# Segment sums in the bank of the used-up edge products, and GpSimd's sums in two pieces

## The chip, the cores and the metric
The kernel runs on one core of a Trainium2 chip. The metric is the device time of one execution in microseconds (us); less is better. The engines of the core run side by side, each with a queue of its own that it works off in order: TensorE (PE in the profile, its weight loads PEld), VectorE (DVE), ScalarE (ACT), GpSimd (POOL) and SyncE (SP, which only issues DMAs). They wait for each other by semaphores. PE writes its results to eight banks of PSUM.

## The reference, cut to what matters
Two message-passing layers over 100,000 nodes of 160 numbers (64 scalars, 32 vectors of 3) and 25,000 edges sorted by destination; each layer has a layer norm and a residual. The first layer:

```python
h = relu(layernorm(x))
f, sc = linear(h, lin1), linear(h, sc_w) * node_attr         # per node, 160 wide
w = silu(edge_scalars @ fc_w1) @ fc_w2                        # per edge, 192 weights
edge_feat = products of f[edge_src], edge_attr and w          # per edge, 384 wide
mid = segment_sum(edge_feat, edge_dst, num_segments=N)
x = x + cos(angle(mid)) * sc + sin(angle(mid)) * lin2(mid)
```

The second layer gathers, multiplies, sums by destination and adds `relu` of it to x. Few nodes have edges: for the others the first layer is the dense part alone (x + sc), and the second adds nothing.

## The kernel before, in words
Three passes follow one another.

**Pass 1** does two things at once, woven together slot by slot. The dense part takes the nodes in U = 98 blocks u of 1024 rows (128 partitions, 8 rows each). The edge part takes the edges in T = 196 tiles n of 128, four tiles to a quad q. A step is one dense block with two tiles, and each step has two slots (h = 0 and 1), one tile and half a block in each. The order inside a step is written out by hand for every engine, and each engine runs its own list (`step` and `slot`), so that several blocks and tiles are in flight.

Dense block u, in order:
- SP loads its rows (`x_all`), DVE takes the moments (L1207) and centres them into `hb` (L1330) and `hr` (L1331).
- PE transposes one half of them in each slot (`dense_tr`, L980 and L981, into bank 0 and columns 0 to 127 of bank 1), ACT copies them with relu (`dense_copy`, L795 and L796).
- One step later PE multiplies (`dense_mm`, L985 and L986), DVE forms x1 (L1354) and the second moments, ACT takes the second root (L779), DVE the inverse (L1370) and the shift `nmr` (L1211).
- ACT writes h1 in two halves of four groups each (`dense_h1`, L774). GpSimd adds each half to x1 in `dense_y` (L651, 640 columns), and SP stores h1 and this output.

Edge tile n, in slots s = n, n+1, and so on:
- Slot n: PE forms the source products and the 192 edge weights in bank 5 or 6 by turns (`p1_source`, ends at L1062). ACT scales the first 160 columns out as `g_e` (L824). DVE multiplies features (`p1_features`, L1421 to L1428); one of its products is kept in columns 352 to 447 of the same bank.
- Slot n+1: PE transposes the features (`p1_feat_t`, L1087, bank 4), ACT copies them (L838).
- Slot n+2: PE forms the message parts in bank 7 (L1048 to L1051), ACT and DVE make the message `v_e` of them (L817, L1402, L1409).
- Slot n+3: `p1_sum` sums the messages by destination: two matmuls, one with the tile's selector matrix `same`, one that carries the tile before on (L1075, L1077), 161 columns wide. They go to columns 256 to 416 of bank 1. ACT copies the result to `tot` (`p1_total`, L832).

Once a quad, DVE builds the selector (L1381), GpSimd centres the gathered edge rows (L655, L656) and issues four indirect gathers (L604), PE transposes these rows (`p1_tr`) into bank 4 and columns 128 to 255 of bank 1, and ACT copies them (L811, L812).

So bank 1 is shared by three users: the rest of the dense transposes, the rest of the edge rows' transposes and the segment sums. While ACT reads one of them out, PE does not write another: `dense_tr` and `p1_tr` wait for `e_tot` (the sums' copy), and `p1_sum` waits for `d_hT` (the copy of the dense transposes).

PE's order in a slot is: dense products of the block before, (once a quad `p1_tr`), feature transposes of tile s-1, message parts of s-2, source products of s, sum of s-3, and then the dense transposes.

**Pass 2** gathers the nodes that have edges and redoes their row with the edge part; **pass 3** runs the second layer over the edges. Both come after pass 1.

Of the kernel before, what the change touches and what calls it, by code (L numbers as in the profile page):

```python
# [19 lines left out]
P = 128  # L20
GD = 8
GQ = 4
D = 160
# [4 lines left out]
CW = D + 1  # L28
# [7 lines left out]


U_C, U_A, U_D, U_B = 0, 32, 97, 193
U_SEG = 2 * P


class At:
# [26 lines left out]
def wait(eng, sem, value):  # L69

    if not (isinstance(value, int) and value <= 0):
        eng.wait_ge(sem, value)  # L72


def gnn_kernel(nc, xa, src, dst, dst_rows, number, edges_in, scalars_in, scalars_t_in, wpack, out):
    f32, i32 = mybir.dt.float32, mybir.dt.int32
    ALU, ACT, AX = mybir.AluOpType, mybir.ActivationFunctionType, mybir.AxisListType
    N = xa.shape[0]
    T = src.shape[1]
    Q = T // GQ  # L80
    UROWS = P * GD
    U = -(-N // UROWS)
# [36 lines left out]
    with ExitStack() as ctx:  # L119
# [3 lines left out]
        def two(name, shape, dt=f32):  # L123
            return [sb(f"{name}{i}", shape, dt) for i in range(2)]
# [4 lines left out]
        def sem(name):  # L129
            return ctx.enter_context(nc.semaphore(name))  # L130
# [4 lines left out]
        bank = [ctx.enter_context(nc.psum_tensor(f"bank{i}", [P, 512], f32)) for i in range(8)]  # L135
# [49 lines left out]
        x1 = two("x1", [P, GD * D])  # L185
        h1 = two("h1", [P, GD * D])
        yo = two("yo", [P, GD * D])
# [7 lines left out]
        same = two("same", [P, GQ * P])  # L195
        carry = two("carry", [P, GQ * P])
# [11 lines left out]
        v_e = two("v_e", [P, CW])  # L208
        tot = two("tot", [P, GQ * CW])
# [59 lines left out]
        d_hT = sem("dense_hT_copied")  # L269
# [8 lines left out]
        d_y = sem("dense_y_ready")  # L278
# [17 lines left out]
        e_ft = sem("p1_features_ready")  # L296
# [7 lines left out]
        e_tot = sem("p1_sum_copied")  # L304
# [283 lines left out]
        def _(pool):  # L588
# [55 lines left out]
            def dense_y(u):  # L644
                j = u.mod(2)
                for h in range(2):
                    pool.wait_ge(d_h1, u.times(2, h + 1))
                    if h == 0:
                        wait(pool, d_sto[j], u.over(2, 16))
                    a, b = h * GQ * D, (h + 1) * GQ * D  # L650
                    nc.gpsimd.tensor_tensor(yo[j][:, a:b], x1[j][:, a:b], h1[j][:, a:b], ALU.add).then_inc(d_y, 1)  # L651

            def centre(into, rest, rows, st, g, signal):
                x = x3(rows, XW, g)
# [111 lines left out]
        def _(act):  # L766
# [60 lines left out]
            def p1_total(n):  # L827
                act.wait_ge(e_seg, n.times(1, 1))
                j, t = n.c // GQ % 2, n.mod(4)
                if t == 0:  # L830
                    wait(act, e_st[j], n.over(8, 16))
                nc.scalar.activation(tot[j][:, t * CW:(t + 1) * CW], bank[1][:, U_SEG:U_SEG + CW],  # L832
                                     ACT.Copy).then_inc(e_tot, 1)

            def p1_feat_t(n):
# [140 lines left out]
        def _(pe):  # L976
            def transpose_rows(main, rest, ps_main, ps_rest, tr_sem):

                for t in range(GQ):
                    nc.tensor.transpose(ps_main[:, t * P:(t + 1) * P], main[:, t * P:(t + 1) * P], ident[:, :])  # L980
                nc.tensor.transpose(ps_rest, rest, ident[:, :]).then_inc(tr_sem, 1)  # L981

            def linear(dst_ps, main, rest, w, t):

                nc.tensor.matmul(dst_ps, main[:, t * P:(t + 1) * P], wp[:, w:w + D], start=True, stop=False)  # L985
                return nc.tensor.matmul(dst_ps[:, 0:DS], rest[:, :], wp[:, w + D + t * DS:w + D + (t + 1) * DS],  # L986
                                        start=False, stop=True)
# [20 lines left out]
            def dense_mm(u, h):  # L1008
                pe.wait_ge(d_hT, u.times(2, h + 1))
                for k in range(GQ):  # L1010
                    if h == 0 and k == 0:
                        pe.wait_ge(d_scl, u.times(1, 1))
                    if k % 2 == 0:
                        wait(pe, d_x1, u.times(4, 2 * h + k // 2 - 1))
                    ins = linear(bank[2 + k // 2][:, k % 2 * D:(k % 2 + 1) * D], hT[h], hR[h], W_SC, k)
                    if k % 2 == 1:
                        ins.then_inc(d_mm, 1)

            def dense_tr(u, h):
                pe.wait_ge(d_cen, u.times(1, 1))  # L1020
                wait(pe, d_hT, u.times(2, h))
                wait(pe, e_tot, u.times(2, h - 2))
                q = At(u.i, u.c // 2, 2) + u.c % 2 * h
                pe.wait_ge(e_hT, q.times(1, 1) if q.within(Q) else Q)
                transpose_rows(hb[u.mod(2)][:, h * 4 * P:(h + 1) * 4 * P], hr[u.mod(2)][:, h * P:(h + 1) * P], bank[0],
                               bank[1][:, 0:P], d_tr)
# [10 lines left out]
            def p1_tr(q):  # L1037
                pe.wait_ge(e_cen, q.times(1, 1))
                wait(pe, e_fte, q.times(GQ, -2))
                wait(pe, d_hT, q.times(4, -1))  # L1040
                wait(pe, e_tot, q.times(4, -4))
                transpose_rows(h_e[:, :], hr_e[:, :], bank[4], bank[1][:, P:2 * P], e_tr)

            def p1_parts(n):
                pe.wait_ge(e_fte, n.times(1, 1))
                wait(pe, e_v, n.times(1))
                f = fT[n.mod(2)]
                nc.tensor.matmul(bank[7][:, U_C:U_C + 97], f[:, 0:P], wp[:, W_R1:W_R1 + 97], start=True, stop=True)  # L1048
                nc.tensor.matmul(bank[7][:, U_D:U_D + 161], f[:, P:2 * P], wp[:, W_R2:W_R2 + 161],
                                 start=True, stop=False)  # L1050
                nc.tensor.matmul(bank[7][:, U_B:U_B + 65], f[:, 2 * P:3 * P], wp[:, W_R3:W_R3 + 65],  # L1051
                                 start=False, stop=True).then_inc(e_u, 1)

            def p1_source(n):
                j, t = n.c // GQ % 2, n.mod(4)
                if t == 0:
                    pe.wait_ge(e_hT, n.over(4, 1, 1))
                    pe.wait_ge(e_hid[j], n.over(8, 16, 16))
                wait(pe, e_ft, n.times(1, -1))
                b = bank[5 + n.mod(2)]  # L1060
                linear(b[:, 0:D], eT[j], eR[j], W_L1, t)
                nc.tensor.matmul(b[:, D:D + 192], q_hid[j][:, t // 2 * P:(t // 2 + 1) * P],  # L1062
                                 wp[:, W_FC2 + t % 2 * 192:W_FC2 + (t % 2 + 1) * 192],
                                 start=True, stop=True).then_inc(e_pw, 1)

            def p1_sum(n, dense_copied):
                j, t = n.c // GQ % 2, n.mod(4)
                if t == 0:
                    pe.wait_ge(e_sc, n.over(4, 1, 1))
                    pe.wait_ge(e_ca[j], n.over(8, 16, 16))  # L1070
                pe.wait_ge(e_v, n.times(1, 1))
                wait(pe, e_tot, n.times(1))
                wait(pe, d_hT, dense_copied)
                before = tot[j][:, (t - 1) * CW:t * CW] if t else tot[1 - j][:, (GQ - 1) * CW:GQ * CW]
                nc.tensor.matmul(bank[1][:, U_SEG:U_SEG + CW], same[j][:, t * P:(t + 1) * P], v_e[n.mod(2)][:, :],  # L1075
                                 start=True, stop=False)
                nc.tensor.matmul(bank[1][:, U_SEG:U_SEG + CW], carry[j][:, t * P:(t + 1) * P], before,  # L1077
                                 start=False, stop=True).then_inc(e_seg, 1)

            def p1_feat_t(n):  # L1080
                pe.wait_ge(e_ft, n.times(1, 1))
                wait(pe, e_fte, n.times(1))
                if n.mod(4) == 2 and (n + 2).within(T):
                    pe.wait_ge(e_hT, (n + 2).over(4, 1, 1))
                f = feat[n.mod(2)]
                for c, at in enumerate((0, 128, 192)):
                    ins = nc.tensor.transpose(bank[4][:, c * P:(c + 1) * P], f[:, at:at + P], ident[:, :])  # L1087
                ins.then_inc(e_ftr, 1)

            def slot(u, h):  # L1090
                s = At(u.i, 2 * u.c + h, 8)
                q1 = At(u.i, u.c // 2, 2) + 1
                if (u - 1).within(U):
                    dense_mm(u - 1, h)
                if h == 1 and u.mod(2) == 1 and q1.within(Q):
                    p1_tr(q1)
                if (s - 1).within(T):
                    p1_feat_t(s - 1)
                if (s - 2).within(T):
                    p1_parts(s - 2)  # L1100
                if s.within(T):
                    p1_source(s)
                if (s - 3).within(T):
                    p1_sum(s - 3, u.times(2, h) if u.within(U) else 2 * U)

            def step(u):
                slot(u, 0)
# [737 lines left out]
```

## Time and profile before
| | |
|---|---|
| median of 3 runs | 2462.75 us (2461.12 to 2464.57) |
| profiled execution | 2464.93 us, its span 2463.1 us |
| busy: PE, DVE, ACT, POOL | 1773.9, 1866.4, 1350.1, 1483.3 us |
| POOL L651, yo sums of 640 columns | 196, mean 1550 ns |
| ACT L832, copy of the segment sums | 196, mean 305 ns |
| PE L980, dense transposes: idle before them | 111.7 us, ended by ACT's copy L832 |

Busy tenths in 40 equal slices of the span, and the granted clock of PE (9 is 90% or more):

```profile
PE   6788888888888888888886544545444777777776
DVE  1799999999999999999996766666664555656554
ACT  2466666666666666666665645555553444444443
POOL 2345455454555545555454777777776777767775
PEclk9999999999999999999998555555555999999999
```

A slice is 61.6 us. The first pass takes the slices up to the twenty-second, the second those in which the clock stands at 5, the third the rest. A row of the timeline gives the start in the span, the duration, the engine, the line, what is written and read, and in brackets how long the engine had been idle and what ended that idle time.

### The profile page before, as it was taken

How to read it: one execution, taken by the hardware profiler on the slowest of the kernel's cores; microseconds unless marked ns; L12 is line 12 of the kernel's file. 1: busy time of each engine (PE TensorE's matmuls, PEld its weight loads, DVE VectorE, ACT ScalarE, POOL GpSimd, SP SyncE). 2: the span in 40 equal slices, each digit the busy share in tenths (PEclk: the TensorE clock that was granted, in tenths of full speed). 3: DMA queues.
4: the chain of work that ended last, by engine and by line, in shares of the span. 5: the costliest groups of instructions: out<-in, count | busy, mean ns of one | idle time of the engine just before them, and what ended most of it. 6: DMA issues, size and time to landing. Idle time of an engine off the chain costs nothing. (4 is left out here: it accounts for less than half of the span.)

```text
span 2463.1 us, 51415 instructions
## 1 busy us (share of the span) xinstructions
PE 1773.9 (72%) x12130; PEld 1620.2 (66%) x12130; DVE 1866.4 (76%) x6716; ACT 1350.1 (55%) x3801; POOL 1483.3 (60%) x1436
## 2 busy tenths in 40 slices
PE   6788888888888888888886544545444777777776
PEld 2777777777777777777775544444444666666665
DVE  1799999999999999999996766666664555656554
ACT  2466666666666666666665645555553444444443
POOL 2345455454555545555454777777776777767775
PEclk9999999999999999999998555555555999999999
DMA  5355555555555555555554333333333333333332
GB/s 184 128 188 206 200 192 193 185 205 200 195 194 184 203 200 198 194 182 202 200 201 165 118 107 113 113 116 121 116 107 93 99 97 105 108 102 109 108 105 72
DMA packets 162656, 376.27 MB, mean 153 GB/s; under 512 B 42142, under 2 KB 72092, under 8 KB 162462
## 3 DMA queue, kind: packets, MB, share of 16 engines
q1 hardware_dynamic: 115582, 301.58, 34.7%
q0 software_dynamic: 47040, 74.31, 11.4%
q8 instruction: 11, 0.18, 0.0%
q14 instruction: 23, 0.19, 0.0%
HBM read 182.72 MB, written 200.80 MB: 156 GB/s over the span
## 5 line engine op out<-in xcount | busy, mean ns | idle before, releaser
L651 POOL TENSOR_TENSOR yo<-x,h 128x640 f32<-128x640 f32 x196 | 303.7, 1550 | 506.0 <-ACT h L774 504.8
L985 PE MATMUL bank<-wp,hT 128*128 128x160 f32 x1568 | 376.3, 322 | 0.0
L774 ACT ACTIVATE h<-x,nmr,inv 128x160 f32<-128x160 f32 x784 | 342.1, 514 | 1.5 <-DVE nmr L1211 1.5
L985 PE MATMUL bank<-wp,eT 128*128 128x160 f32 x784 | 263.6, 429 | 49.9 <-ACT eR L897 43.7
L610 POOL DMA_INDIRECT out<-yo,i_put x196 | 209.1, 1067 | 119.2 <-issue 80.7
L604 POOL DMA_INDIRECT x_e<-in_xa,i_src x196 | 217.3, 1109 | 98.7 <-issue 47.2
L1354 DVE SCALAR_TENSOR_TENSOR x<-bank,scl,x_all 128x160 f32<-128x160 f32 x784 | 256.3, 365 | 5.1 <-PE bank L986 2.6
L610 POOL DMA_INDIRECT h_all<-h,i_put x196 | 223.9, 1142 | 59.8 <-issue 58.6
L986 PE MATMUL bank<-wp,hR 128*128 128x64 f32 x1568 | 259.3, 247 | 0.0
L986 PEld LDWEIGHTS bank<-wp,hR 128*128 128x128 f32 x1568 | 255.5, 190 | 0.0
L980 PE MATMUL bank<-ident,h_e 128*128 128x128 f32 x392 | 83.6, 351 | 223.4 <-DVE hr_e L1526 223.0
L949 ACT ACTIVATE tot<-bank 128x160 f32<-128x160 f32 x196 | 59.8, 305 | 333.0 <-PE bank L1181 333.0
L985 PEld LDWEIGHTS bank<-wp,hT 128*128 128x128 f32 x1568 | 237.7, 192 | 4.2 <-issue 4.2
L795 ACT ACTIVATE hT<-bank 128x512 f32<-128x512 f32 x196 | 117.1, 597 | 209.5 <-PE bank L981 209.5
L738 POOL DMA_INDIRECT h<-h_all,i_src x196 | 194.1, 990 | 61.8 <-issue 57.6
L604 POOL DMA_INDIRECT x_all<-in_xa,i_dst x196 | 194.4, 992 | 59.6 <-issue 59.0
L1715 DVE TENSOR_TENSOR xr<-bank,q_ed 128x96 f32<-128x96 f32 x196 | 50.5, 258 | 235.9 <-PE bank L1169 235.9
L1159 PE MATMUL bank<-ident,feat 128*128 128x128 f32 x392 | 87.2, 305 | 182.4 <-DVE feat L1708 156.0
L1207 DVE BATCH_NORM_STATS2 st<-x 128x6 f32<-128x320 f32 x490 | 217.9, 485 | 0.0
L980 PEld LDWEIGHTS bank<-ident,h_e 128*128 128x128 f32 x392 | 58.0, 185 | 232.3 <-DVE hr_e L1526 215.0
L985 PEld LDWEIGHTS bank<-wp,eT 128*128 128x128 f32 x784 | 163.9, 259 | 69.3 <-issue 36.8
L980 PE MATMUL bank<-ident,hb 128*128 128x128 f32 x784 | 124.5, 282 | 111.7 <-ACT tot L832 111.7
(163 smaller groups left out, 5537.8 us busy)
## 6 DMA issues: line engine op xcount, KB each, us to landing
x_all<-in_xa SPq DMA_DIRECT2D x98, 644.0 KB, 5.0
h_all<-h SPq DMA_DIRECT2D x98, 640.0 KB, 3.0
out<-yo SPq DMA_DIRECT2D x98, 640.0 KB, 3.4
q_row<-row_tab SPq DMA_DIRECT2D x98, 256.0 KB, 3.6
sum_tab<-tot SPq DMA_DIRECT2D x49, 322.0 KB, 4.2
y_tab<-yo SPq DMA_DIRECT2D x49, 320.0 KB
x<-y_tab SPq DMA_DIRECT2D x49, 320.0 KB
cv<-sum_tab SPq DMA_DIRECT2D x25, 322.0 KB, 3.1
```

The costliest lines, as they stand in the source:

```text
L604: nc.gpsimd.indirect_dma_start(into[:, t * width:(t + 1) * width], None, rows, bass.IndirectOffsetOnAxis(ap=index[:, t:t + 1], axis=0)).th ...
L610: nc.gpsimd.indirect_dma_start(rows, bass.IndirectOffsetOnAxis(ap=index[:, t:t + 1], axis=0), tile, None, bounds_check=N - 1, oob_is_err=F ...
L651: nc.gpsimd.tensor_tensor(yo[j][:, a:b], x1[j][:, a:b], h1[j][:, a:b], ALU.add).then_inc(d_y, 1)
L738: nc.gpsimd.indirect_dma_start(h1[j][:, t * D:(t + 1) * D], None, h1_all, bass.IndirectOffsetOnAxis(ap=i_src[j][:, t:t + 1], axis=0)).then ...
L774: ins = nc.scalar.activation(h1[j][:, k * D:(k + 1) * D], x1[j][:, k * D:(k + 1) * D], ACT.Relu, bias=nmr2[j][:, k:k + 1], scale=inv2[j][: ...
L795: nc.scalar.activation(hT[h][:, :], bank[0][:, :], ACT.Relu)
L980: nc.tensor.transpose(ps_main[:, t * P:(t + 1) * P], main[:, t * P:(t + 1) * P], ident[:, :])
L985: nc.tensor.matmul(dst_ps, main[:, t * P:(t + 1) * P], wp[:, w:w + D], start=True, stop=False)
L986: return nc.tensor.matmul(dst_ps[:, 0:DS], rest[:, :], wp[:, w + D + t * DS:w + D + (t + 1) * DS], start=False, stop=True)
L1159: nc.tensor.transpose(b[:, c * P:(c + 1) * P], f[:, c * P:(c + 1) * P], ident[:, :])
L1207: return V.bn_stats(st[:, 2 * pair:2 * pair + 2, :].rearrange("p g k -> p (g k)"), two_rows[:, 0:D, :])
L1354: ins = V.scalar_tensor_tensor(x1[j][:, k * D:(k + 1) * D], bank[2 + pair % 2][:, k % 2 * D:(k % 2 + 1) * D], scl1[u.mod(4)][:, k:k + 1], ...
```

## The change
The sums of tile n go to columns 0 to 160 of bank 5 or 6, into the bank in which the source products of tile n+2 stood. The bank changes hands by two new waits. `p1_sum(n)` waits until DVE's features of tile n+2 are done, the last reader of these products. `p1_source(n)` waits until ACT has copied the sum of tile n-4, which stood in the bank that it writes. ACT's copy reads from there. The waits for `e_tot` go from `dense_tr` and `p1_tr`, the one for `d_hT` from `p1_sum`.

On GpSimd each half of the output block, 640 columns in one instruction, becomes two instructions of 320 columns, and the semaphore is raised by the second.

```diff
@@ dense_y, GpSimd
-                    a, b = h * GQ * D, (h + 1) * GQ * D
-                    nc.gpsimd.tensor_tensor(yo[j][:, a:b], x1[j][:, a:b], h1[j][:, a:b], ALU.add).then_inc(d_y, 1)
+                    for k in (2 * h, 2 * h + 1):
+                        a, b = 2 * k * D, 2 * (k + 1) * D
+                        ins = nc.gpsimd.tensor_tensor(yo[j][:, a:b], x1[j][:, a:b], h1[j][:, a:b], ALU.add)
+                    ins.then_inc(d_y, 1)
@@ p1_total, ScalarE
-                nc.scalar.activation(tot[j][:, t * CW:(t + 1) * CW], bank[1][:, U_SEG:U_SEG + CW],
+                nc.scalar.activation(tot[j][:, t * CW:(t + 1) * CW], bank[5 + n.mod(2)][:, 0:CW],
@@ dense_tr, TensorE
-                wait(pe, e_tot, u.times(2, h - 2))
@@ p1_tr, TensorE
-                wait(pe, e_tot, q.times(4, -4))
@@ p1_source, TensorE
+                wait(pe, e_tot, n.times(1, -3))
@@ p1_sum, TensorE
-            def p1_sum(n, dense_copied):
+            def p1_sum(n):
-                wait(pe, d_hT, dense_copied)
+                pe.wait_ge(e_ft, n.times(1, 3) if (n + 2).within(T) else T)
+                total = bank[5 + n.mod(2)][:, 0:CW]
-                nc.tensor.matmul(bank[1][:, U_SEG:U_SEG + CW], same[j][:, t * P:(t + 1) * P], v_e[n.mod(2)][:, :],
+                nc.tensor.matmul(total, same[j][:, t * P:(t + 1) * P], v_e[n.mod(2)][:, :],
-                nc.tensor.matmul(bank[1][:, U_SEG:U_SEG + CW], carry[j][:, t * P:(t + 1) * P], before,
+                nc.tensor.matmul(total, carry[j][:, t * P:(t + 1) * P], before,
```

## Rows read from the trace of the kernel before

**Rows 1.** DVE's line L1354: durations (min/median/max, ns), first and last start.
```profile
L1354 DVE SCALAR_TENSOR_TENSOR x<-bank,scl,x_all x784: 321/371/388, 81.8 to 1325.0; 128x160 f32<-128x160 f32 x196
```

**Rows 2.** Busy by engine from 146 to 1240 us: PE, PEld, DVE, ACT, POOL, clock, DMA.
```profile
146.00:1240.00 1094.00, 915.17 (x7046) 859.06 (x7045) 1013.12 (x3084) 704.91 (x1965) 571.96 (x555) 1.00 0.55 196
```

**Rows 3.** Waits from 85 to 1320 us: who for whom, total us, times, longest.
```profile
PE bank L980 <- ACT tot L832: 111.7, 193, 0.8
...
DVE bank L1421 <- ACT g_e L824: 51.0, 96, 0.8
...
PE bank L1087 <- ACT eR L812: 47.3, 48, 1.0
...
DVE inv L1370 <- ACT sd L779: 36.4, 47, 1.1
```

**Rows 4.** Timeline, DVE: the feature products that waited for g_e.
```profile
800.50 0.27 DVE L1421 TENSOR_TENSOR bank<-bank,g_e 128x96 f32<-128x96 f32 x1 [0.33 <-ACT g_e L824]
...
807.87 0.27 DVE L1421 TENSOR_TENSOR bank<-bank,g_e 128x96 f32<-128x96 f32 x1 [0.78 <-ACT g_e L824]
...
826.03 0.27 DVE L1421 TENSOR_TENSOR bank<-bank,g_e 128x96 f32<-128x96 f32 x1 [0.25 <-ACT g_e L824]
...
851.73 0.27 DVE L1421 TENSOR_TENSOR bank<-bank,g_e 128x96 f32<-128x96 f32 x1 [0.33 <-ACT g_e L824]
```

**Rows 5.** Timeline, PE: the feature transposes in S4.
```profile
823.48 0.55 PE L1087 MATMUL bank<-ident,feat 128*128 128x128 f32 x3 [0.90 <-DVE feat L1428]
```

**Rows 6.** Timeline, all engines: from the transposes of S2 to the shift.
```profile
809.39 0.60 ACT L795 ACTIVATE hT<-bank 128x512 f32<-128x512 f32 x1 [1.10 <-PE bank L981]
...
811.88 1.54 POOL L651 TENSOR_TENSOR yo<-x,h 128x640 f32<-128x640 f32 x1 [2.19 <-ACT h L774]
...
812.02 0.20 DVE L1370 RECIPROCAL inv<-sd 128x8 f32<-128x8 f32 x1 [1.09 <-ACT sd L779]
...
812.71 0.73 DVE L1211 SCALAR_TENSOR_TENSOR nmr<-st,inv 128x8 f32<-128x8 f32 x1
```

**Rows 7.** Timeline, PE: the sum products at the end of S2, the transposes of S3.
```profile
812.92 0.44 PE L1075 MATMUL bank<-v_e,same 128*128 128x161 f32 x2
...
813.20 0.44 PE L1077 MATMUL bank<-tot,carry 128*128 128x161 f32 x2
...
814.23 0.30 PE L980 MATMUL bank<-ident,hb 128*128 128x128 f32 x1 [0.59 <-ACT tot L832]
```

**Rows 8.** Groups of POOL's instructions, 146 to 1240 us: busy us, mean ns, idle before.
```profile
L651 POOL TENSOR_TENSOR yo<-x,h 128x640 f32<-128x640 f32 x171 | 264.1, 1544 | 433.6 <-ACT h L774 432.6
...
L671 POOL TENSOR_TENSOR scl_e<-inv_e,x_e 128x4 f32<-128x4 f32 x43 | 8.7, 202 | 3.4
```

**Rows 9.** Timeline: a sum of GpSimd and DVE's centring in S3.
```profile
817.64 1.54 POOL L651 TENSOR_TENSOR yo<-x,h 128x640 f32<-128x640 f32 x1 [4.22 <-ACT h L774]
...
818.22 2.04 DVE L1330 TENSOR_TENSOR hb<-x_all,st 128x1024 f32<-128x1024 f32 x1
```

**Rows 10.** Lines L1330, L1331, L1381 from 146 to 1240 us: durations in ns (min/median/max).
```profile
L1330 DVE TENSOR_TENSOR hb<-x_all,st x86: 1211/1634/2190, 152.0 to 1239.8; 128x1024 f32<-128x1024 f32 x86
...
L1331 DVE TENSOR_TENSOR hr<-x_all,st x85: 410/412/419, 154.1 to 1230.0; 128x256 f32<-128x256 f32 x85
...
L1381 DVE TENSOR_TENSOR same<-q_row,f_dst x42: 678/1792/2203, 168.4 to 1218.7; 128x512 f32<-128x512 int32 x42
```

**Rows 11.** Timeline: two shifts of the next pair, and GpSimd's centring beside the second.
```profile
838.46 0.63 DVE L1211 SCALAR_TENSOR_TENSOR nmr<-st,inv 128x8 f32<-128x8 f32 x1
...
850.27 0.16 DVE L1211 SCALAR_TENSOR_TENSOR nmr<-st,inv 128x8 f32<-128x8 f32 x1
...
850.36 1.05 POOL L655 TENSOR_TENSOR h_e<-x_e,st_e 128x512 f32<-128x512 f32 x1
```

**Rows 12.** Timeline: a sum that was started while hb (1291.07, 1.21 us) ran.
```profile
1291.10 2.58 POOL L651 TENSOR_TENSOR yo<-x,h 128x640 f32<-128x640 f32 x1 [2.15 <-ACT h L774]
...
1292.20 1.76 DVE L1331 TENSOR_TENSOR hr<-x_all,st 128x256 f32<-128x256 f32 x1
```

More of the change, by code:

```diff
@@ L38 @@
 U_C, U_A, U_D, U_B = 0, 32, 97, 193
-U_SEG = 2 * P
 class At:
@@ L1103, in slot @@
                 if (s - 3).within(T):
-                    p1_sum(s - 3, u.times(2, h) if u.within(U) else 2 * U)
+                    p1_sum(s - 3)
             def step(u):
```

## The prediction
> **What bounds the kernel now.** I read the page's slices first (the table above): VectorE (DVE) stands at 9 tenths from the second slice to the twenty-first, TensorE (PE) at 8, GpSimd and ScalarE lower. Everything that the diff touches runs there. DVE's x1 of the dense blocks, the frame of the first pass, goes from 81.8 to 1325.0 us [rows 1]: 1243 us of 2463. Passes 2 and 3 execute the same instructions after the change, so I take them as they are. From 146 to 1240 us DVE is busy for 1013 of 1094 us and PE for 915, at a granted clock of 1.00 [rows 2]. Neither is full, so next I read who waits for whom [rows 3]. PE waits 193 times for ScalarE's copy of the segment sums (L832), 112 us in all, nearly every slot: this is what the diff goes at. DVE's waits are for ScalarE's g_e (51 us) and for the second root (36 us).
>
> Whether the 112 us are worth anything is decided by the loop that closes between the engines. DVE takes up the same feature product at 800.50, 826.03 and 851.73 us [rows 4]: the pattern repeats every two steps, in 25.53 and 25.70 us. I call this a pair, 25.6 us; 1243 / 25.6 = 48.6 pairs. PE's stretches in a pair are named by the dense transposes that open them: S1 at 801.18, S2 at 808.54, S3 at 814.23, S4 at 819.91, S1 again at 826.70. All five look like the one at 814.23 [rows 7]: 0.59 or 0.60 us of idle, ended by the copy of the sums. Followed by what ends last, the loop is this:
> - In S4 PE waits 0.90 us for DVE's features; its transposes start at 823.48, the source products follow without a pause [rows 5], then it waits for the sums' copy and opens S1.
> - In S1 it waits about 1 us for ScalarE's copy of the transposed edge rows (L812; 47.3 us in 48 times [rows 3]), goes on to the end of S1 and waits for the sums' copy once more.
> - S2 opens at 808.54. ScalarE copies what was transposed (809.39), normalises and takes the root, and only then DVE, which had waited 1.09 us, gets on at 812.02 [rows 6].
> - From there DVE has no wait until its features are done, just ahead of 823.48: 11.4 us.
> So two of the four sum waits of a pair, those that open S1 and S2, lie on the loop. Those that open S3 and S4 don't, since PE waits for DVE in S4 anyway.
>
> **The bank edit.** It takes the e_tot wait out of the dense transposes and of p1_tr, and the d_hT wait out of p1_sum. It adds to p1_source a wait for total n-4, which ScalarE copies in the slot before; on PE the next dense transposes, four dense products and the message parts stand in between, most of a slot of 5.7 us. It adds to p1_sum a wait for the features of tile n+2, which p1_feat_t awaited earlier in the same slot of the same queue. Both cost nothing. The first would cost if ScalarE fell a slot behind: then the source product, the sum and the next transposes would stand behind the waiting instruction, and DVE's g_e with them. ScalarE's copy reads as many columns from another bank: nothing.
>
> What one wait is worth: the second pair of sum products starts at 813.20, the transposes at 814.23. From the first pair to the second it is 0.28 us, so without the wait the transposes could start at 813.48, 0.75 us earlier; 0.59 of it is shown as idle, the rest is pipeline that the stop empties [rows 7]. Bounds 0.59 and 0.75; I take 0.75, the spacing of PE's own neighbours. Nothing takes the wait's place at once: ScalarE idles 1.10 us for these transposes [rows 6]. Two waits are 1.50 us a pair. Does DVE let that through? It waits 1.09 us ahead of the root, 0.78 ahead of g_e in S1 (807.87) and 0.25 in S4 (826.03), 2.12 us in this pair [rows 4, 6]. One sum wait lies ahead of the 0.78, which is just used up. The chain through PE and ScalarE stays the later one, barely.
>
> **The split.** A sum of 640 columns takes 1.54 us, an operation on 4 columns 0.20 [rows 8]. A line through both (2.1 ns a column) gives 0.87 us for 320, two are 1.74, 0.20 more than one. GpSimd idles 2.19 and 4.22 us ahead of sums [rows 6, 9], so that extra is hidden; without that cover it would be 4 x 0.20 us a pair on GpSimd alone. The worth lies on DVE, whose instructions with both inputs in SBUF are stretched while a sum runs. The shift (nmr) of 812.71 takes 0.73 us and ends with the sum of 811.88 [rows 6]; unhindered it takes 0.16 [rows 11]. The centring hb of 818.22 takes 2.04 behind the sum of 817.64 [rows 9], at best 1.21; the selector, 0.68 at best, takes 1.79 at the median; the second centring, hr, is never stretched, 0.41 to 0.42 us [rows 10]. That is 0.57 + 0.83 + 1.11 = 2.5 us a pair. Who goes next when both wait is in the trace too. A sum that was started while hb ran got the port as hb ended, took 2.58 us by its record, and hr waited it out, 1.76 us [rows 12]. And the shift of 850.27 had its turn between the end of a sum and the next GpSimd instruction, recorded from 850.36, without being stretched [rows 11]. They take turns, instruction by instruction.
>
> The Trainium skill ("SBUF — State Buffer", section "Who interferes with whom") says that a DVE instruction with two SBUF inputs and a GpSimd instruction that reads SBUF exclude each other for a whole instruction, and that the second to issue blocks. By rows 6, 9 and 10 the trace agrees. Who comes next it doesn't say; read as "first issued, first served", both halves would go ahead of a waiting DVE instruction, which is the second rival below.
>
> With turns taken, counted from S2's start (DVE's root at 3.48 as now):
> - nmr: DVE arrives at 4.17; the first half runs from 3.34 to 4.21, so nmr waits 0.04 us instead of 0.57. The margin is as thin: where nmr comes at 838.46 and ends with the sum of 837.53 [rows 11], the first half would end at 838.40, and nmr would wait out the second, 0.8 us instead of 0.47.
> - hb and hr: the sum of S3 comes 0.75 us earlier, at 8.34. If nmr was spared, hb arrives at 9.11, waits 0.10 and runs; then the second half has its turn and hr waits 0.87: 0.97 instead of 0.83. If nmr was held, hb arrives at 9.9, waits 0.2, and hr nothing. Either way DVE's 11.4 us shrink by about 0.4.
> - The selector waits 0 to 0.87 us (now 1.11 at the median). It lies ahead of the root's wait and only keeps DVE from becoming the later chain. The second nmr may meet GpSimd's centring behind the sum (1.05 us [rows 11]), which comes earlier now: 0.1 us on the loop.
> Net 0.3 us a pair; -0.5 if each meeting goes badly, +1.4 if nmr and hb are not held at all (0.57 + 0.83).
>
> **The sum.** (1.50 + 0.3) x 48.6 = 87 us, off the profiled execution's 2464.93 (span 2463.1): 2377. That execution lies 2.2 us above the median of 2462.75, so **2375 us**. With 0.59 for a wait and -0.5 for the split it is 0.68 x 48.6 = 33 us (2430); with +1.4 it is 141 (2322), and DVE, whose unhindered work is 1013 / 1094 x 25.6 - 2.5 = 21.2 us a pair [rows 2], would hardly wait any more.
>
> **Rivals.**
> - **Small gain, 5 to 50 us.** The split takes back part: the halves follow so closely that DVE waits out both, or hb and hr are each held by a half and nmr too. For it: margins of 0.04 us, and a sum that moves up against hb. Against it: turns are taken [rows 11, 12]. With -0.5 and 0.59: 2430.
> - **The split does nothing**, since both halves are served as one: 1.50 x 48.6 = 73 us, 2390. Inside my range.
> - **Slower, the port becomes the bound.** If nmr, hb and hr each meet a half (2.61), the selector both (1.74) and the second nmr the centring (1.05), it is 5.4 us of stretching a pair; DVE alone needs 21.2 + 5.4 = 26.6 us, 1.0 more than the pair has now: +49 us, 2512. It decides from 4.4 us of stretching; now it is 2.5.
> - **No change: the copy isn't the releaser.** If PE's stop were another wait of the same transposes (centred rows, previous copy), nothing would move: 2463. Against it: hb of 818.22 ended at 820.26 [rows 9] and its rows are transposed from 826.70 on, and the previous copy lies a slot back.
> - **More than 125 us**, if DVE is no longer held: 2322.
>
> **Chances.** Forecast with the variant at 2390 (2340 to 2412) 0.80; small gain beyond it 0.09; above 125 us 0.04; no change 0.03; slower 0.04. So 2340 to 2412 holds 8 in 10. About 0.2% (5 us) is what a measurement of this kernel can tell from no change: faster 0.93, same 0.03, slower 0.04.
>
> **What would show it.** Right: no wait of L980 for L832; a pair of 23.8 us; DVE's wait for g_e in S1 near 0, ahead of the root 0.3 to 0.5; PE's wait for the features in S4 up from 0.90 to about 2; halves of 0.87 us; hr stretched in many pairs. Wrong: DVE without any wait (then it is the bound, and its stretching the price), halves far from 0.87, nmr held for 0.8 or more everywhere, a new wait of PE for L832 in p1_source, or passes 2 and 3 of another length.

## The result, and the profile after
The changed kernel takes **2380.86 us** (median of 4 runs, 2377.11 to 2390.95) against 2463.02 before (4 runs): a ratio of 0.9671, 95% interval 0.9655 to 0.9687. 2375 had been forecast, with 2340 to 2412 as the range. The execution shown below took 2377.11 us, its span is 2375.3.

The slices first, as in the table of before:
```profile
PE   6888888888888888989885445454445777777776
DVE  2799999999999999999987666666664566555564
PEclk9999999999999999999995555555557999999999
```
The first pass ends one and a half slices earlier, the other two have kept their shape. DVE's x1 (now L1355) runs from 81.7 to 1240.0 us: 84.9 us less than in [rows 1]. What follows the last x1 takes 1135.3 us instead of 1138.1. So 85 of the 88 us between the two spans come from the first pass. 1158.3 us are 48.6 pairs of 23.8 us.

The waits from 85 to 1280 us (who for whom, total us, times, longest), to be held against [rows 3]:
```profile
PE bank L1088 <- DVE feat L1429: 86.9, 49, 2.7
...
ACT hT L796 <- PE bank L982: 59.1, 194, 0.3
...
PE bank L1088 <- ACT eR L813: 47.3, 48, 1.0
...
DVE bank L1422 <- ACT g_e L825: 29.7, 51, 1.6
...
DVE inv L1371 <- ACT sd L780: 15.7, 17, 1.4
```
PE's 112 us for the copy of the sums are gone, and ScalarE waits 0.3 us for the dense transposes instead of 1.10. PE's wait for the features in S4 has doubled. DVE's two waits have shrunk from 87 to 45 us, and the one ahead of the root comes 17 times instead of 47.

The windows of the stretch from 146 to 1160 us (PE, PEld, DVE, ACT, POOL busy, PE's granted clock, DMA):
```profile
146.00:1160.00 1014.00, 893.46 (x6993) 878.70 (x6992) 965.01 (x3056) 697.61 (x1950) 610.73 (x722) 0.98 0.59 209
```
DVE is busy for 95% of it (93% in [rows 2]). The clock is 0.98 on average where it was 1.00.

DVE's instructions with two SBUF inputs (ns, min/median/max), from 146 to 1160 us, and GpSimd's pieces over the whole span, to be held against [rows 8] and [rows 10]:
```profile
L1382 DVE TENSOR_TENSOR same<-q_row,f_dst x42: 683/2140/2230, 162.7 to 1142.2; 128x512 f32<-128x512 int32 x42
...
L1331 DVE TENSOR_TENSOR hb<-x_all,st x85: 1202/1227/1262, 146.4 to 1151.0; 128x1024 f32<-128x1024 f32 x85
...
L1332 DVE TENSOR_TENSOR hr<-x_all,st x85: 406/416/431, 147.6 to 1152.1; 128x256 f32<-128x256 f32 x85
...
L1212 DVE SCALAR_TENSOR_TENSOR nmr<-st,inv x85: 159/451/869, 152.0 to 1156.5; 128x8 f32<-128x8 f32 x85
...
L651 POOL TENSOR_TENSOR yo<-x,h x392: 852/862/2255, 98.4 to 1248.3; 128x320 f32<-128x320 f32 x196
```
A stretched instruction is one that takes longer than its best because GpSimd's sum runs beside it. hb is no longer stretched here, hr isn't either, and nmr is about as before. Summed over the first pass as the time above the best duration, nmr has 0.7 us a pair where it had 0.6. The selector is stretched more than before by its median (2.14 us, 1.79 before), but by its sum it has 1.0 us a pair as before, for it is nearly spared in the pairs with a dip of the clock, which come below.

Two meetings from the timeline show why:
```profile
686.86 1.68 POOL L651 TENSOR_TENSOR yo<-x,h 128x320 f32<-128x320 f32 x2
...
686.97 2.13 DVE L1382 TENSOR_TENSOR same<-q_row,f_dst 128x512 f32<-128x512 int32 x1
...
694.17 1.70 POOL L651 TENSOR_TENSOR yo<-x,h 128x320 f32<-128x320 f32 x2 [3.29 <-ACT h L775]
...
695.70 1.25 DVE L1331 TENSOR_TENSOR hb<-x_all,st 128x1024 f32<-128x1024 f32 x1
```
The selector waits out both pieces (686.86 + 1.68 = 688.54, and it ends 0.56 us later). The sum of S3 starts 1.53 us ahead of hb, where it was 0.58 in [rows 9], and ends 0.17 us after hb's start (694.17 + 1.70 = 695.87).

One thing was in no forecast. Of 46 pairs (from one nmr to the second next) 15 or so take 25.0 us and nearly all of the others 23.3 to 23.4, in a pattern that repeats every third pair for most of the pass. Two neighbours in PE's timeline:
```profile
676.75 0.55 PE L1088 MATMUL bank<-ident,feat 128*128 128x128 f32 x3 [1.83 <-DVE feat L1429]
...
677.33 0.47 PE L1048 MATMUL bank<-wp,fT 128*128 128x161 f32 x2
...
700.16 0.75 PE L1088 MATMUL bank<-ident,feat 128*128 128x128 f32 x3 [1.83 <-DVE feat L1429]
...
701.08 0.80 PE L1048 MATMUL bank<-wp,fT 128*128 128x161 f32 x2
```
Both start after the same 1.83 us of idle time, but the products behind the second take 1.7 times as long. The windows show the granted clock (the third figure from the end):
```profile
654.00:678.00 24.00, 21.22 (x173) 20.88 (x173) 23.71 (x76) 16.96 (x47) 15.00 (x18) 1.00 0.60 209
701.00:702.00 1.00, 1.00 (x7) 1.00 (x6) 1.00 (x5) 0.43 (x1) 0.96 (x2) 0.50 0.29 84
```
For some 3.4 us PE runs at 0.50, which is 1.2 GHz instead of 2.4, right where DVE waits for what comes of it (g_e, up to 1.6 us). I call such a stretch a dip. The kernel before idled 0.90 us at this place [rows 5] and had none of it.

### The profile page after: what moved, and what is told of

Same layout as the page of the kernel before. It is cut to its first block and busy times, and to the rows that moved or that the text cites. A ratio compares the mean times of both kernels' runs of the same rounds, so it can differ in the third digit from the quotient of the medians.

```text
span 2375.3 us, 51586 instructions
## 1 busy us (share of the span) xinstructions
PE 1754.5 (74%) x12130; PEld 1646.7 (69%) x12130; DVE 1821.5 (77%) x6716; ACT 1348.1 (57%) x3801; POOL 1528.5 (64%) x1632
## 5 line engine op out<-in xcount | busy, mean ns | idle before, releaser
L651 POOL TENSOR_TENSOR yo<-x,h 128x320 f32<-128x320 f32 x392 | 333.6, 873 | 373.2 <-ACT h L775 372.1
L986 PE MATMUL bank<-wp,eT 128*128 128x160 f32 x784 | 268.9, 436 | 49.8 <-ACT eR L898 43.7
L603 POOL DMA_INDIRECT x_e<-in_xa,i_src x196 | 234.9, 1199 | 98.8 <-issue 64.9
L1355 DVE SCALAR_TENSOR_TENSOR x<-bank,scl,x_all 128x160 f32<-128x160 f32 x784 | 252.4, 365 | 3.4 <-POOL yo L651 2.7
L1160 PE MATMUL bank<-ident,feat 128*128 128x128 f32 x392 | 86.8, 304 | 182.0 <-DVE feat L1709 155.5
L1088 PE MATMUL bank<-ident,feat 128*128 128x128 f32 x588 | 106.1, 292 | 134.4 <-DVE feat L1429 87.2
L1160 PEld LDWEIGHTS bank<-ident,feat 128*128 128x128 f32 x392 | 39.8, 142 | 214.2 <-DVE feat L1709 140.4
```

What stands on the lines that cost most here:

```text
L603: nc.gpsimd.indirect_dma_start(into[:, t * width:(t + 1) * width], None, rows, bass.IndirectOffsetOnAxis(ap=index[:, t:t + 1], axis=0)).th ...
L651: ins = nc.gpsimd.tensor_tensor(yo[j][:, a:b], x1[j][:, a:b], h1[j][:, a:b], ALU.add)
L1160: nc.tensor.transpose(b[:, c * P:(c + 1) * P], f[:, c * P:(c + 1) * P], ident[:, :])
L1355: ins = V.scalar_tensor_tensor(x1[j][:, k * D:(k + 1) * D], bank[2 + pair % 2][:, k % 2 * D:(k % 2 + 1) * D], scl1[u.mod(4)][:, k:k + 1], ...
```

## The experiments
The questions were: what each half of the change is worth, whether the long idle stretch of PE in S4 is what brings the clock down, and what stretches the selector. Times are medians of 4 or 5 runs; ratios are to the kernel before, run on the same chip. Kernels of different series ran on different chips, so there the ratios compare better than the times.

| kernel | us | ratio (95%) | dips of the clock | pair, us |
|---|---|---|---|---|
| changed | 2380.9 | 0.9671 (0.9655 to 0.9687) | 15 | 23.9 |
| bank edit alone | 2383.0 | 0.9679 (0.9663 to 0.9695) | 21 | 24.0 |
| split alone | 2441.0 | 0.9911 (0.9894 to 0.9928) | 0 | 25.1 |
| changed, waits back for even blocks | 2379.8 | 0.9666 (0.9650 to 0.9682) | 0 | 23.9 |
| bank edit, the same waits | 2384.8 | 0.9685 (0.9669 to 0.9701) | 0 | 24.0 |
| changed, first sum after gather 1 | 2408.8 | 0.9790 (0.9773 to 0.9806) | 23 | 24.6 |
| changed, first sum after gather 2 | 2409.5 | 0.9768 (0.9713 to 0.9822) | 21 | 24.6 |
| changed, first sum ahead of the gathers | 2484.9 | 1.0102 (1.0080 to 1.0124) | 33 | 26.2 |
| bank edit, whole sum after gather 1 | 2378.5 | 0.9667 (0.9651 to 0.9683) | 18 | 23.9 |
| changed, PE kept busy in S4 | 2352.6 | 0.9562 (0.9546 to 0.9578) | 0 | 23.4 |
| whole sum after gather 1, PE kept busy | 2347.3 | 0.9541 (0.9522 to 0.9560) | 0 | 23.2 |
| whole sum after gather 1, waits back | 2378.9 | 0.9668 (0.9652 to 0.9684) | 0 | 23.9 |
| bank edit, PE kept busy | 2350.9 | 0.9554 (0.9541 to 0.9567) | 0 | 23.3 |

Dips are counted as the stretches of the first pass in which the granted clock stands at 0.50. A pair is the mean distance of every second nmr in the first pass, to 0.1 us.

**The bank edit alone.**
```diff
-                    for k in (2 * h, 2 * h + 1):
-                        a, b = 2 * k * D, 2 * (k + 1) * D
-                        ins = nc.gpsimd.tensor_tensor(yo[j][:, a:b], x1[j][:, a:b], h1[j][:, a:b], ALU.add)
-                    ins.then_inc(d_y, 1)
+                    a, b = h * GQ * D, (h + 1) * GQ * D
+                    nc.gpsimd.tensor_tensor(yo[j][:, a:b], x1[j][:, a:b], h1[j][:, a:b], ALU.add).then_inc(d_y, 1)
```


> The bank edit alone; GpSimd's sums stay at 640 columns. Theory (the split is worth nothing, because DVE's selector waits out both halves, 2.13 us in the changed kernel's trace, as it waited out the whole sum): time within 10 us of the changed kernel, 2370 to 2385 us, hb unstretched too because the sum of S3 now ends before hb starts, selector and nmr stretched by about 0.15 us a pair less. Rival (the halves spare DVE 0.3 us a pair, as my prediction has it): 14 us slower than the changed kernel, about 2395.

2382.95 us, 2 more than with the split, as the theory has it. The whole sum now starts 1.36 us ahead of hb and hb isn't stretched; DVE's stretching is 1.5 us a pair. The intervals of the two ratios overlap: beside the bank edit the split can't be told from nothing. The clock blurs this comparison (21 dips against 15); the last experiment makes it with the clock held.

**The split alone** (the kernel before with the split's lines only).

> The split alone; banks and waits as before. Theory (DVE waits out both halves, and two halves take 1.70 us instead of 1.54): hb and nmr, both on the loop, are stretched up to 0.16 us more each, 2463 to 2478 us. Rival (turns are taken): nmr spared 0.5 us in half of the pairs and hb held by halves one at a time, 2445 to 2460 us.

2441.02 us, 21 us faster than before, and both expectations missed. Timelines of the sum and of hb in S3:
```profile
626.42 3.06 POOL L652 TENSOR_TENSOR yo<-x,h 128x320 f32<-128x320 f32 x2 [4.03 <-ACT h L776]
...
627.21 1.20 DVE L1332 TENSOR_TENSOR hb<-x_all,st 128x1024 f32<-128x1024 f32 x1
```
hb comes 0.79 us after the first piece has started, just at its end, goes ahead unstretched, and the second piece waits for it: 3.06 us for two pieces. So here a turn was taken, and hb's stretching falls from 0.87 us a pair to 0.09. Part of it is given back in a place that I had called hidden: DVE's x1 waits 19 times, 52 us in all, for GpSimd's sum of the block before. So the split has a worth of its own, but largely the same one that the bank edit takes by moving the sum away from hb; their gains (21 and 79 us) don't add up (82).

**Waits put back for the even blocks.** They cut PE's idle stretch in S4.
```diff
                 wait(pe, d_hT, u.times(2, h))
+                if u.c % 2 == 0:
+                    wait(pe, e_tot, u.times(2, h - 2))
```


> The changed kernel with the old wait for the sums' copy put back into the dense transposes of the even blocks, those that open S3 and S4. They lie off the loop: PE waits for DVE's features in S4 anyway. In the changed kernel PE idles 1.83 us at one go there in every pair, and in every third pair the granted clock falls to 0.50 for some 3.4 us and the pair takes 25.0 instead of 23.35 us. Theory (the long idle stretch is what brings the clock down): with the idle time cut up into 0.6 us pieces the clock stays at 1.00, 16 x 1.65 = 26 us less than the changed kernel, about 2355. Rival (it is the sum of idle time, or something else): the dips stay, 2381; or the waits cost by themselves, 2390 or more.

2379.78 us. The clock stayed at 1.00 and no dip is left, as the theory has it, but the time is the same (2355 was expected). PE is no busier than in the changed kernel, 889 us of this stretch against 893, so it isn't the sum of its idle time that brings the clock down:
```profile
146.00:1160.00 1014.00, 889.06 (x7002) 855.60 (x7001) 947.98 (x3058) 696.96 (x1953) 634.06 (x719) 1.00 0.59 209
```
The longest idle stretch that recurs in S4 is 1.3 us now. A new wait has taken the place of the dips:
```profile
689.55 0.68 DVE L1384 TENSOR_TENSOR same<-q_row,f_dst 128x512 f32<-128x512 int32 x1
...
691.07 2.50 POOL L651 TENSOR_TENSOR yo<-x,h 128x320 f32<-128x320 f32 x3
...
692.88 0.38 DVE L1357 SCALAR_TENSOR_TENSOR x<-bank,scl,x_all 128x160 f32<-128x160 f32 x1 [2.65 <-POOL yo L651]
```
In every second pair the selector comes early enough to pass ahead of the sum unstretched (0.68), and then the x1 behind it, which overwrites what the sum reads, waits for the sum all the same, 24 times 2.65 us. As a test of the clock's price this run says nothing; as a test of what brings it down it speaks for the length of the idle stretch.

With whole sums:

> As the kernel before it (waits put back for even blocks), with GpSimd's sums of 640 columns. Theory (split worth nothing, clock held): 2350 to 2357 us, no dip of the clock. Rival (split spares 0.3 us a pair): 14 us slower than with the split.

2384.76 us, where 2350 to 2357 was expected. The picture is the same: no dip, 24 waits for the sum, 60.7 us. It is 5 us slower than with the split, and the runs of the two kernels don't overlap: here the split is worth something, though a third of the 14 us of the rival.

**The first sum among the gathers.** The sum behind the selector sits behind four gathers on GpSimd's queue, though its input is ready earlier. It is moved up.
```diff
+                early = w.mod(2) == 0 and (q + 1).within(Q) and (w - 3).within(U)
                 if w.mod(2) == 0 and (q + 1).within(Q):
-                    p1_gather(q + 1)
+                    p1_gather(q + 1, 1 if early else None, lambda: dense_y(w - 3, (0,)))
                 if (w - 3).within(U):
-                    dense_y(w - 3)
+                    dense_y(w - 3, (1,) if early else (0, 1))
```
`p1_gather` calls the function ahead of gather 1 (after the first); 2 and 0 in the two other kernels.

> The changed kernel with one move on GpSimd: in the steps with edge gathers the first half block's sum (two pieces) is issued after the first of the four gathers instead of after the fourth. In the changed kernel this sum starts at 686.86 us, right behind the gathers, though its input was ready at 682.5; DVE's selector (686.97, 2.13 instead of 0.68 us) ends with it, and in the kernels of the first series DVE's next x1 waits 2.65 us for it outright. Theory (what stretches the selector is GpSimd coming late: the x1 behind it would wait for this sum anyway): stretching and wait go from 1.1 us a pair to nearly 0, DVE gets shorter, PE's wait in S4 falls below 1.83 us and with it the dips of the clock go: pair of 22.3 to 22.8 us instead of 23.9, 2315 to 2330 us. Rival (port turns: the sum only meets another instruction of DVE's, hb or hr of S1, and stretches that): 2370 to 2385.

> As the kernel before it, with the sum after the second gather. It then falls into the stretch between DVE's hr and its selector. Theory: as good as after the first or better by the stretching that hr or hb has there, 2312 to 2330 us. Rival: 2370 to 2385.

> As the two before it, with the sum ahead of all four gathers. It meets hb of S1 (1.21 us) and the gathers are 1.7 us later, whose rows DVE needs more than 10 us after. Theory: DVE waits at hb up to 0.9 us in every pair, 10 to 40 us slower than after the second gather, still faster than the changed kernel. Rival: 2370 to 2385.

2408.77, 2409.48 (one of its four runs took 2387.99) and 2484.91 us: all slower than the changed kernel, the last slower than the kernel before. No expectation was met. The selector's stretching is gone (0.0, 0.1 and 0.0 us a pair), as expected, and x1 doesn't wait; but the sums now meet hb, hr and nmr. From the kernel with the sum after gather 1:
```profile
503.15 1.69 POOL L653 TENSOR_TENSOR yo<-x,h 128x320 f32<-128x320 f32 x2
...
503.18 2.75 DVE L1334 TENSOR_TENSOR hb<-x_all,st 128x1024 f32<-128x1024 f32 x1
```
and from the one with the sum ahead of the gathers, the other half block's sum and nmr:
```profile
513.10 1.99 DVE L1215 SCALAR_TENSOR_TENSOR nmr<-st,inv 128x8 f32<-128x8 f32 x1
...
513.38 1.68 POOL L653 TENSOR_TENSOR yo<-x,h 128x320 f32<-128x320 f32 x2
```
Both wait out two pieces, 1.5 and 1.8 us. The second meeting is odd in that nmr is recorded 0.28 us ahead of the sum and yet ends with it (515.09 and 515.06).

These meetings alone don't explain the loss. All four instructions together are stretched by 1.8, 1.3 and 2.3 us a pair, against 1.8 in the changed kernel: only the last kernel has more. What has grown in all three is the clock's share. In the kernel with the sum after gather 2 the first pass takes 1192.7 us, 34 more than in the changed kernel, though DVE is busy for 10 us less (1092 against 1102):
```profile
81.50:1274.20 1192.70, 1051.06 (x8029) 1030.92 (x8030) 1091.74 (x3493) 799.61 (x2227) 736.74 (x813) 0.96 0.56 199
```
The meetings are unevenly spread. A pair of 22.74 us, in which PE idles 1.08 us in S4, is followed by one in which it idles 2.66. Where the clock holds that second pair takes 24.56 us, with a dip of 3.4 us it takes 26.2, with one of 6.8 us 27.4. The two pairs without a dip make 23.65 us on average, 0.3 more than the undisturbed pair of the changed kernel (some 15 us in the pass). The rest of the 34, some 20 us by this estimate, is the clock's: 21 dips, of which 10 last 6.8 us. The other two kernels have 23 and 33 dips, of which 10 and 16 last 6.8 us.

**The same move with whole sums.**

> The bank edit and the moved sum (after the first gather), with sums of 640 columns in one instruction: the split undone where GpSimd no longer comes late. Theory (split worth nothing beside the bank edit): within 6 us of the kernel with the two pieces. Rival (turns at the piece boundary spare DVE): slower by 10 us or more, with hb, hr or nmr stretched by up to 1.5 us each.

2378.51 us, 30 us faster than with two pieces. hb is stretched 0.84 us a pair, hr and the selector never. Neither expectation was met: in this place the split is a loss. Most of it is the clock's: 18 dips, all of 3.4 us, where the kernel with two pieces has 23, ten of them twice as long. At 1.65 us for each 3.4 us at 0.50 that is 15 x 1.65 = 25 of the 30 us, an estimate. What the split costs or gives here with the clock held was not run.

**PE kept busy in S4.** Eight transposes of the identity are put ahead of the wait for the features. They write where the feature transposes write next, so their result is overwritten, and the wait for the previous copy out of that bank (`e_fte`) has to come ahead of them. Nothing else is moved.
```diff
             def p1_feat_t(n):
+                wait(pe, e_fte, n.times(1))
+                if n.mod(4) == 1 and n.within(T):
+                    for _ in range(8):
+                        nc.tensor.transpose(bank[4][:, 0:P], ident[:, :], ident[:, :])
                 pe.wait_ge(e_ft, n.times(1, 1))
-                wait(pe, e_fte, n.times(1))
```


> The changed kernel, with eight transposes of the identity put on PE's queue in S4 ahead of the features' wait (into columns of bank 4 that the feature transposes then overwrite; no result depends on them). Nothing else moves: PE waits 1.83 us there anyway, eight transposes take about 0.9. Theory (the granted clock falls to 0.50 in every third pair because PE idles 1.83 us at one go in S4, and that costs the pair 1.65 us): the clock stays at 1.00, 15 dips go, 25 us less than the changed kernel, about 2355. Rival (the dips come from something else, the engine's load or the time since the last one): they stay, 2381.

2352.60 us, 28 less than without (27 by the ratios); 2355 was expected. No dip is left. The windows, 146 to 1160 us:
```profile
146.00:1160.00 1014.00, 928.18 (x7493) 908.71 (x7493) 997.61 (x3121) 711.80 (x1991) 617.16 (x739) 1.00 0.59 213
```
The clock is 1.00, and DVE is busy for 98.4% of the time: it is the bound. This run holds the answer to both questions on the clock: with idle stretches of 0.95 us in S4 it stays at 1.00, and the 15 dips cost about what was expected of them (15 x 1.65 = 25 us).

> The same eight transposes in the kernel with whole sums of 640 columns, the first of which is issued after the first gather; it had 18 dips and pairs of 23.2 us without one. Theory: no dips, pair of 23.2 us, 18 x 1.65 = 30 us less than that kernel, about 2349. Rival: 2378.

2347.33 us, 31 less than without; 2349 was expected. It has the lowest median of the study, but the intervals of its ratio and of those of the two other kernels with PE kept busy overlap.

> The same kernel (whole sums, first one after the first gather) with the old waits for the sums' copy put back into the dense transposes of the even blocks instead. In the first series these waits took the dips away, and the gain went into DVE's wait for GpSimd's sum behind the gathers (2.65 us in every second pair), which can't come here. Theory: no dips and no such wait, pair of 22.9 to 23.3 us, 2340 to 2355. Rival (the waits shift the sum of S3 against hb and cost by themselves): 2375 or more.

2378.85 us: missed. No dip and no wait for the sum, but the waits put back shift the sums so that hb is stretched twice a pair, 1.7 us in all, and nmr 0.9. The rival had that. What paid here was to fill the idle stretch without moving ScalarE's work, as the eight transposes do.

**The bank edit alone, PE kept busy.**

> The bank edit alone (sums of 640 columns, as before, behind the gathers) with the eight transposes in S4: the changed kernel's split undone where the clock doesn't blur the comparison. The pairs of the bank edit alone that had no dip took 23.2 to 23.3 us, those of the changed kernel 23.3 to 23.4. Theory (split worth nothing beside the bank edit, slightly more time on GpSimd): 2344 to 2351 us, against 2352.6 with the split. Rival (the split spares DVE 0.3 us a pair once the clock is held): 2362 to 2370.

2350.86 us (5 runs), ratio 0.9554 (0.9541 to 0.9567), against 0.9562 (0.9546 to 0.9578) with the split. The stretching of DVE is 2.0 us a pair against 2.1. The theory holds. The split's 0.3 us a pair, 14 us, are excluded in this place; a difference of 2 us can't be told from none.

## Why the prediction was right
**The waits: right.** PE no longer stops ahead of the dense transposes. They open S2, S3 and S4 of a pair at 685.89, 690.79 and 695.69 us:
```profile
690.79 0.60 PE L981 MATMUL bank<-ident,hb 128*128 128x128 f32 x4
...
695.69 0.60 PE L981 MATMUL bank<-ident,hb 128*128 128x128 f32 x4
```
S2 and S3 take 4.90 us each where S2 took 5.69 (from 808.54 to the 814.23 of [rows 7]): 0.79 a wait, forecast 0.75 and not the 0.59 that the profile shows as idle. The added waits cost nothing: PE waits for the sums' copy nowhere. That two of the four waits lie on the loop fits S4, where PE waits 1.83 us; "about 2" was forecast. It was not tested by itself: no run puts back the waits of S1 and S2 alone, and those of S3 and S4 changed the phase of GpSimd's sums as well.

**"The chain through PE and ScalarE stays the later one, barely": wrong.** This step failed, inside a total that came out. DVE is the bound in most pairs: it waits ahead of the root 17 times instead of 47, and with the clock held it is busy for 98.4%. Of a pair of 23.4 us that is 23.0, of which 2.1 are stretching: 20.9 us of its own work, where I had worked out 21.2, and 0.4 us of waits. "DVE without any wait (then it is the bound, and its stretching the price)" had been named as a sign of being wrong, and the undisturbed pairs come close to it.

**The sum and hb: half right.** I had the sum of S3 0.75 us earlier against hb, still in its way. It was 0.95 us (0.58 to 1.53 ahead), and hb got free: its stretching fell from 0.87 to 0.06 us a pair. That isn't the split's doing: in the kernel with the bank edit alone the whole sum starts 1.36 us ahead of hb and doesn't hold it either. hr, forecast to be held, wasn't in the stretch shown.

**The split: wrong for the selector and nmr, right for hb where it meets one, and nothing in the sum.** Two pieces take 1.70 us (forecast 1.74), but the selector isn't let in between them: it waits both out, 1.46 us at the median (forecast 0 to 0.87, before 1.11), and so does nmr in the kernels in which it starts in the first half microsecond of the first piece. hb does get the turn that I had counted on. From the kernel with the sum after gather 1:
```profile
479.92 2.66 POOL L653 TENSOR_TENSOR yo<-x,h 128x320 f32<-128x320 f32 x2 [2.87 <-ACT h L778]
...
480.20 1.66 DVE L1334 TENSOR_TENSOR hb<-x_all,st 128x1024 f32<-128x1024 f32 x1
...
481.78 1.08 DVE L1335 TENSOR_TENSOR hr<-x_all,st 128x256 f32<-128x256 f32 x1
```
hb waits 0.45 us, for the first piece only, the second piece waits for hb, and hr waits for the second piece (1.08 instead of 0.41 us): the forecast picture. In the changed kernel hb comes after both pieces, and the turn has nothing to give. The variant "the split does nothing" (2390) is what the runs show: 2381 with and 2383 without it, 2352.6 and 2350.9 with the clock held. The split alone does gain 21 us, mostly by the turn that goes to hb (0.87 to 0.09 us a pair).

**"That extra is hidden": not always, without effect here.** The one x1 that waited for a sum before (1.9 us) was the sign of a margin nearly used up. In the changed kernel the selector's stretching covers it (the x1 behind it would wait for the same sum); where the selector is spared, x1 waits 2.65 us. The wait isn't the split's own: it comes 24 times with whole sums too (60.7 against 64 us).

**The clock: missing.** No rival had it. I had forecast that PE's wait in S4 would double, and read the clock's 1.00 as given. The dips give back 25 us by their count, 28 by the run with PE kept busy, of a gain that would have been 110.

So the 82 us measured against 88 forecast hold two errors that cancel: an undisturbed pair is 2.25 us shorter instead of 1.8 (23.3 to 23.4 us against the 23.8 forecast), and the clock takes back 0.5. I put the 0.45 us more down to hb, which got free; no run shows it by itself. The total lies well inside the range; that it lies so close to 2375 is luck.

## What to carry to other kernels
When a wait is taken from an engine that waits for the bound anyway, its idle time doesn't vanish but gathers in one place. On PE, ask how long that stretch becomes, and fill it with work that nobody reads if the clock falls behind it. Here eight transposes gave 28 us, a third of the gain again. GpSimd's sums cost DVE by where they meet its instructions with two SBUF inputs, and every shift of phase deals these meetings anew: count on the sum over all of them, and measure each placement. Don't count on a cut instruction to let the other engine in: it did for one instruction here, and not for two others. Before a slower time is put down to such meetings, look at the granted clock. A single short wait in the profile can mark a margin that the next edit uses up.

## What the runs showed of the hardware
- In the changed kernel PE's granted clock fell to 0.50 (1.2 GHz) for some 3.4 us at idle stretches of 1.83 us, though PE was busy for 88% of the time, and only in about every third pair. All 131 dips in the first passes of the six kernels that have any lie at idle stretches of 1.67 us or more; those of 6.8 us lie at stretches of 2.66 us or more. In the kernels whose idle stretches in S4 are of 0.8 to 1.3 us, single ones apart, it never fell, and the one before the change, at 84% busy, is among them. What decides in which pair it falls stays open. The Trainium skill ("TensorE: Matmul & The Clock Gate", section "HAM oscillation — how this bites in real kernels") describes such oscillation for a kernel with far more idle time; here much shorter gaps were enough.
- Who goes next, DVE or GpSimd's second piece, isn't settled by "in turns", and not by the time of arrival alone. In the first passes of all kernels with two pieces, the selector and nmr waited out both pieces in all 125 cases in which they started 0.01 to 0.74 us after the first (selector, 0.11 us after: 2.13 us instead of 0.68). hb, started 0.03 us after or less, waited out both in one kernel (2.75 us) and went ahead of both in another. Where it started 0.04 to 0.70 us after, it waited for the first piece alone in 79 of 82 cases (0.28 us after: 1.66 us, the pieces 2.66). At the end of the first piece, 0.79 us after its start, it went ahead without a wait (1.20 us, the pieces 3.06). What sets hb apart stays open.
- A GpSimd sum of 320 columns takes 0.86 us where 640 take 1.54. By a line through both, 0.18 us a piece don't depend on the length.
